# Seven-product query projection: two token blocks kept in place, output weights elsewhere, three value tiles moved behind the first products

## What is computed

```python
queries = (q @ Wq.T).reshape(B, Sq, NHEADS, HEAD_DIM).transpose(0, 2, 1, 3)
keys = (k @ Wk.T).reshape(B, Skv, KVHEADS, HEAD_DIM).transpose(0, 2, 1, 3)
values = (v @ Wv.T).reshape(B, Skv, KVHEADS, HEAD_DIM).transpose(0, 2, 1, 3)
queries = _rope(queries)
keys = _rope(keys)
...
attn = jax.nn.softmax(scores, axis=-1)
ctx = jnp.einsum('bhqk,bhkd->bhqd', attn, values)
ctx = ctx.transpose(0, 2, 1, 3).reshape(B, Sq, NHEADS * HEAD_DIM)
return ctx @ Wd.T
```

## Time and profile before

| what | value |
|---|---|
| median of 3 runs | 738.43 us (737.69 to 738.82) |
| the profiled execution | 738.54 us, of which the span is 736.7 us |
| granted TensorE clock, mean | 0.998 |
| TensorE busy | 710.8 us, 96% of the span |
| VectorE, GpSimd, ScalarE busy | 520.8, 485.9, 371.9 us |
| moved by DMA | 51.09 MB, mean 69 GB/s |

### The profile page before, as it was taken

One profiled execution on the slowest core, in us unless ns is written; L12 is line 12 of the kernel. 1 busy time (PEld: TensorE's weight loads), 2 busy tenths in 40 slices (PEclk: granted clock), 3 DMA queues, 4 the chain that ended last, 5 costly groups with the idle time before them and its releaser, 6 DMA issues.

```text
span 736.7 us, 12893 instructions
## 1 busy us (share of the span) xinstructions
PE 710.8 (96%) x4848; PEld 565.4 (77%) x4848; DVE 520.8 (71%) x815; ACT 371.9 (50%) x555; POOL 485.9 (66%) x366
## 2 busy tenths in 40 slices
PE   9999997799999999999999999989999999999897
PEld 7788886567787778787778778767787888877786
DVE  5756857766756757767757757757667887888855
ACT  5456645635544644743653554544246776653220
POOL 1898535678777776867867867746325799964440
PEclk9999999999999999999999999999999999999999
DMA  7553514031211310311301212200200110020003
GB/s 271 206 172 132 172 51 133 17 129 44 86 44 44 107 49 17 113 41 43 100 28 44 98 43 72 73 16 15 87 1 1 44 59 2 2 87 1 15 1 114
DMA packets 25561, 51.09 MB, mean 69 GB/s; under 512 B 2352, under 2 KB 10672, under 8 KB 25520
## 3 DMA queue, kind: packets, MB, share of 16 engines
q1 hardware_dynamic: 25520, 50.53, 20.8%
HBM read 40.04 MB, written 10.49 MB: 69 GB/s over the span
## 4 chain that ended last, share of the span: by engine, by line
PE 79%; DVE 7%; POOL 6%; ACT 3%; issue 3%; DMA 1%; SPq 0%; DVEq 0%; POOLq 0%
PE pj L1517 11%; PE sc L1610 9%; PE pj L1610 9%; PE pj L1708 8%; PE tp L1517 7%; PE pv L1503 6%; PE pv L1597 4%; PE tp L1610 4%; PE sc L1577 3%; PE tp L1491 2%; PE pj L1491 2%; PE sc L1758 2%; PE tp L1584 2%; PE tp L1771 2%; PE pv L1782 2%
## 5 line engine op out<-in xcount | busy, mean ns | idle before, releaser
L482 POOL TENSOR_TENSOR sw<-sw,cst 128x512 f32<-128x512 f32 x72 | 100.6, 1398 | 38.3 <-ACT sw L655 38.2
L1517 PE MATMUL pj<-x,w 128*128 128x512 f32 x384 | 103.5, 406 | 1.0 <-ACT pc L693 0.6
L506 POOL TENSOR_TENSOR sm<-sm,mx 128x512 f32<-128x512 f32 x64 | 72.0, 1131 | 45.5 <-DVE mx L1166 26.4
L1517 PEld LDWEIGHTS pj<-x,w 128*128 128x128 f32 x384 | 69.4, 189 | 24.6 <-DVE cq L1089 4.9
L500 POOL TENSOR_TENSOR w<-raw,w 128x896 fp32r<-128x896 f32 x28 | 60.9, 2196 | 34.6 <-ACT w L640 34.6
L511 POOL TENSOR_TENSOR sm<-sm,rz 128x512 f32<-128x512 f32 x64 | 65.9, 1043 | 19.5 <-DVE rz L1181 19.5
L1517 PE MATMUL tp<-x,w 128*128 128x512 f32 x288 | 76.2, 401 | 2.6 <-ACT sw L655 1.4
L488 POOL TENSOR_TENSOR qr<-t,sw 128x512 f32<-128x512 f32 x54 | 73.3, 1358 | 7.7
L775 ACT ACTIVATE sm<-sm 128x512 f32<-128x512 f32 x64 | 40.2, 631 | 69.2 <-POOL sm L506 69.2
L1708 PE MATMUL pj<-xh,ws 128*128 128x512 f32 x192 | 64.3, 401 | 0.2 <-ACT kb L863 0.2
L1517 PEld LDWEIGHTS tp<-x,w 128*128 128x128 f32 x288 | 51.9, 188 | 13.3 <-ACT sw L655 1.7
(11 more groups left out here) (268 smaller groups left out, 1799.3 us busy)
## 6 DMA issues: line engine op xcount, KB each, us to landing
rawd<-in_w_d SPq DMA_DIRECT2D x16, 512.0 KB, 3.3
raw<-in_w_q SPq DMA_DIRECT2D x15, 512.0 KB, 3.3
kscr<-sm SPq DMA_DIRECT2D x16, 256.0 KB, 2.2
vscr<-sm SPq DMA_DIRECT2D x16, 256.0 KB, 2.6
kr<-kscr SPq DMA_DIRECT2D x8, 512.0 KB, 3.3
vv<-vscr SPq DMA_DIRECT2D x16, 256.0 KB, 2.6
raw<-in_w_k SPq DMA_DIRECT2D x4, 512.0 KB, 6.2
cT<-in_ctxT SPq DMA_DIRECT2D x4, 512.0 KB, 7.4
```

The costliest lines, as they stand in the source:

```text
L482: pool.tensor_tensor(bs(sw[par][:, :]), bs(sw[par][:, :]), rep(cst[:, C_SIN:C_SIN + S], HB), ALU.mult).then_inc(sin_done, 1)
L506: pool.tensor_tensor(s3, s3, per_group(mx[:, c, :], 8), ALU.subtract).then_inc(subbed, 1)
L1517: last = pe.matmul(bank, a, r, start=(start and k == 0 and part == 0), stop=(stop and k == 1 and part == 2), skip_group_check=True)
```

## The change

Blocks 5 and 6 of the tokens are no longer in `x7`: their high and low parts are written into `xt`, which covers `cT`, on the quarters whose contents are no longer needed; the low part overwrites its own source. `wdh` and `wdl` take the place that these blocks had in `x7`, and the fourth `t1` temporary of the first queries becomes `t1x`, a place that value tiles 13 to 15 don't read. These three tiles go behind the first queries' products. `first_add(2)` and (3) come before (4) and (5), so head 0 waits for six sums instead of four. `w7_sum(2)` moves from between `block_lo(4)` and `block_lo(5)` to behind `first_t1(5)`. `kr` is loaded ahead of the last four value spills. A `memset` of `kb[0]`, which lies where `wdl` is now, waits for another count. The rest of the diff follows from these.

```diff
@@ -97,15 +97,17 @@
 
 
         xs = ExitStack()
-        x7 = sb(xs, "x7", [P, 7, 2, 1024], F32R)
+        x7 = sb(xs, "x7", [P, 5, 2, 1024], F32R)
+        wdh = sb(xs, "wdh", [P, REP, D], F32R)
+        wdl = sb(xs, "wdl", [P, REP, D], F32R)
         w7 = [sb(xs, f"w7{i}", [P, 2, 7 * 256], F32R) for i in range(2)]
         qr = sb(xs, "qr", [P, B, REP, S])
         kr = sb(xs, "kr", [P, B, S])
         cq = [sb(xs, f"cq{i}", [P, HALF]) for i in range(2)]
         u2 = sb(xs, "u2", [P, HALF])
         pc = sb(xs, "pc", [P, HALF])
-        wdh = sb(xs, "wdh", [P, REP, D], F32R)
-        wdl = sb(xs, "wdl", [P, REP, D], F32R)
+
+        xt = sb(xs, "xt", [P, KT, TOK], F32R)
         ch = sb(xs, "ch", [P, 2, 8, P], F32R)
         cl = sb(xs, "cl", [P, 2, 8, P], F32R)
         vv = sb(xs, "vv", [P, HB, DH])
@@ -132,6 +134,11 @@
         sb(f2, "gap_f2", [P, 100 * 256])
         raw8b = sb(f2, "raw8b", [P, 8, 256])
         f2.close()
+
+        f3 = ExitStack()
+        sb(f3, "gap_f3", [P, 136 * 256])
+        t1x = sb(f3, "t1x", [P, HALF])
+        f3.close()
         pcb, u2b = sm4[0], sm4[1]
         kst, vst = sm4[0:2], sm4[2:4]
 
@@ -273,6 +280,9 @@
         x7src = [xblock(0, 0), xblock(1, 0), xblock(1, 1), xblock(0, 0), xblock(1, 1), xblock(0, 1), xblock(1, 0)]
 
         def x7b(i, hl):
+            if i >= 5:
+                kh, h = (((1, 1), (0, 1)), ((0, 0), (1, 0)))[i - 5][hl]
+                return xt[:, 2 * kh:2 * kh + 2, h * HALF:(h + 1) * HALF]
             return x7[:, i, hl, :].rearrange("p (k t) -> p k t", k=2)
 
         def q_out(p, k):
@@ -325,7 +335,7 @@
 
         FIRST = [(0, 0), (1, 0), (0, 1), (1, 1), (0, 2), (1, 2), (0, 3), (1, 3)]
 
-        t1f, swf = t1 + pt, sw + swx
+        t1f, swf = t1 + [pt[0], t1x], sw + swx
 
         block = es.enter_context(nc.Block())
 
@@ -401,20 +411,21 @@
                     sp.wait_ge(wlo, 2)
                     sp.wait_ge(wsum, 6)
                     load_q(1, 0)
-
-            for i in range(2):
-                sp.wait_ge(s_ks[i], 16 * NKT // 2)
-            sp.wait_ge(wlo, 4)
-            load_kr(0)
+                if vi == 11:
+                    for i in range(2):
+                        sp.wait_ge(s_ks[i], 16 * NKT // 2)
+                    sp.wait_ge(wlo, 4)
+                    load_kr(0)
+
             sp.wait_ge(vproj, NVT)
             for i in range(2):
                 load_d(0, i)
+            sp.wait_ge(wlo, 6)
+            load_q(1, 1)
             for i in range(2):
                 sp.wait_ge(s_vs[i], 16 * NVT // 2)
             for i in range(2):
                 load_vv(0, i)
-            sp.wait_ge(wlo, 6)
-            load_q(1, 1)
 
             def head(g, last):
                 if not last:
@@ -536,8 +547,8 @@
                 first_add(i, i)
             for i in range(2, 6):
                 first_sin(i)
-            first_add(2, 4)
-            first_add(3, 5)
+            first_add(2, 2)
+            first_add(3, 3)
             first_sin(6)
             first_sin(7)
 
@@ -589,7 +600,7 @@
             late_lo(0)
             late_lo(1)
             late_lo(2)
-            pool.wait_ge(stp, 7 * N_PAIR)
+            pool.wait_ge(outx, 8 * (NKV - 1))
             pool.memset(kb[0][:, :, :, :], 0.0).then_inc(zeroed, 1)
             late_lo(3)
             ln_pow(2)
@@ -678,8 +689,8 @@
                     act.wait_ge(ln_cp, NT)
                 else:
                     act.wait_ge(tdone, (1, 3, 2, 4)[i - 3])
-                if i == 5:
-                    act.wait_ge(vproj, NVT)
+                if i >= 5:
+                    act.wait_ge(x_done, 5)
                 hi(x7src[i], x7b(i, 0), x7hi)
 
             def w7_hi(m, p, raw, free):
@@ -753,12 +764,9 @@
             first_swap(0, C_BANK)
             v_copy(12)
             first_swap(1, T_BANK)
-            v_copy(13)
+            block_hi(5)
             part_copy(u2, 5, A_BANK)
             part_copy(u2b, 6, B_BANK)
-            v_copy(14)
-            v_copy(15)
-            block_hi(5)
             block_hi(6)
             part_copy(pc, 7, C_BANK)
             part_copy(pcb, 8, T_BANK)
@@ -767,8 +775,11 @@
             first_swap(4, A_BANK, None, 1)
             first_swap(5, B_BANK, None, 2)
             w7_hi(2, 0, raw8, 13)
-            first_swap(6, C_BANK, None, 5)
-            first_swap(7, T_BANK, None, 6)
+            v_copy(13)
+            first_swap(6, C_BANK, None, 3)
+            v_copy(14)
+            first_swap(7, T_BANK, None, 4)
+            v_copy(15)
 
             def exp(n, c, scale):
                 act.wait_ge(subbed, n + 1)
@@ -1132,7 +1143,6 @@
                 dve.wait_ge(cadd, 1 + p)
                 first_t1(p, c)
             block_lo(4)
-            w7_sum(2)
             block_lo(5)
             block_lo(6)
             dve.wait_ge(wlo, 4)
@@ -1143,16 +1153,17 @@
             for p, a in enumerate((A_BANK, A2)):
                 dve.wait_ge(stp, 11 + p)
                 first_t1(4 + p, a, 1 + p)
-            first_add(4, 2)
+            w7_sum(2)
             c_add(13, 3, C_BANK, u2)
-            first_add(5, 3)
+            dve.wait_ge(cadd, 5)
+            first_t1(6, C_BANK, 3)
+            first_add(4, 4)
+            first_add(5, 5)
+            c_add(14, 4, C2, u2b)
+            dve.wait_ge(cadd, 6)
+            first_t1(7, C2, 4)
             w7_lo(2, 0, 0)
-            c_add(14, 4, C2, u2b)
-            dve.wait_ge(cadd, 5)
-            first_t1(6, C_BANK, 5)
             w7_lo(2, 0, 1)
-            dve.wait_ge(cadd, 6)
-            first_t1(7, C2, 6)
             first_add(6, 6)
             first_add(7, 7)
             for i in range(2):
@@ -1512,7 +1523,7 @@
             def product(bank, p, w, xb, start, stop):
                 for k in range(2):
                     wh, wl = (w7[p][:, i, w * 256 + k * P:w * 256 + (k + 1) * P] for i in range(2))
-                    mh, ml = (x7[:, xb, i, k * HALF:(k + 1) * HALF] for i in range(2))
+                    mh, ml = (x7b(xb, i)[:, k, :] for i in range(2))
                     for part, (a, r) in enumerate(((wh, mh), (wh, ml), (wl, mh))):
                         last = pe.matmul(bank, a, r, start=(start and k == 0 and part == 0),
                                          stop=(stop and k == 1 and part == 2), skip_group_check=True)
@@ -1541,13 +1552,10 @@
                 product(a, p, W_11, X_11, True, False).then_inc(stp, 1)
                 product(c, p, W_12, X_21, True, True).then_inc(stp, 1)
             v_tile(12)
-            v_tile(13)
             for p, a in enumerate((A_BANK, A2)):
                 pe.wait_ge(x_done, 5)
                 pe.wait_ge(pcp, 1 + p)
                 product(a, p, W_S2, X_T2, False, False).then_inc(stp, 1)
-            v_tile(14)
-            v_tile(15)
             for p, c in enumerate((C_BANK, C2)):
                 pe.wait_ge(swp, Q0 + 1 + p)
                 product(c, p, W_S1, X_T1, True, False).then_inc(stp, 1)
@@ -1562,6 +1570,8 @@
             for p, c in enumerate((C_BANK, C2)):
                 pe.wait_ge(pcp, 5 + p)
                 product(c, p, W_S4, X_22, False, True).then_inc(stp, 1)
+            for i in range(13, NVT):
+                v_tile(i)
 
             def scores_x(g, j, held=False):
                 h, c = j // 2, j % 2
@@ -1620,7 +1630,7 @@
                     pe.wait_ge(x_done, XD0 + 8 * g + j + 1)
 
                 m = 2 * n
-                pe.wait_ge(rope, Q0 + 4 if first else ri(m, 0))
+                pe.wait_ge(rope, Q0 + 6 if first else ri(m, 0))
                 pe.wait_ge(s_kr, 16 * (g + 1))
                 scores_x(g, 0)
                 scores_x(g, 1)
```

## The result

The changed kernel took 732.73 us (median of 6 runs, 731.85 to 733.41), the kernel before, beside it, 738.44 (737.59 to 739.23): a ratio of 0.9923, 95% interval 0.991 to 0.9936. Forecast were 731.0 us, 729.6 to 734.4, and a gain of 7.5 us; the gain is 5.7. The sign and the mechanism came out, the size was 1.8 us too large. The time lies in the range, but 0.2 above what I had given for case A (729.6 to 732.5) and so in the part that I had given to rival B, the chain that doesn't compress. What that says is worked out behind the experiments.

What follows compares the result with a forecast made beforehand. TensorE's idle time, with head 0's first mask on VectorE as the instruction that sets S1, was taken as the bound. Mask at 123.4 for 130.91, 7.5 us earlier: 738.5 - 7.5 = 731.0 us, range 729.6 to 734.4.

Steps and rivals of the forecast that it cites:

- case A: The forecast itself: first mask at 123.4 for 130.91, 7.5 us gained; 729.6 to 732.5 us, chance 0.68.
- rival B: Chain from `c_add` to `first_add(7)` hides nothing, `w7_sum` adds 4.6: gain 3.7 us; 732.5 to 736.9, chance 0.22.
- What bounds it: TensorE's idle time around head 0's start; VectorE's first mask, at 130.91, sets S1 7.40 us later.
- Parts 1 and 2: Value tiles 13 to 15 behind S4, blocks 5 and 6 written elsewhere: S3 at 102.9, 8.4 us earlier.
- part 2: Token blocks 5 and 6 written where the tokens lie, `block_lo` 1.22 us each: costs nothing, covered by S1's 2.72.
- Rival D: Matmuls reading blocks 5 and 6 from their new place cost more; 0.1 us each gives 750; chance 0.04.
- Part 3: Rotary chain on VectorE moves 8.4 us earlier with S3; `w7_sum(2)` put in takes 4.65; `first_add(7)` done at 122.9.
- Part 4: ScalarE's queue: `v_copy(15)` ends at 120.7, last value spill lands at 123.3 and decides the mask by 0.4 us.
- Part 5: SP's loads: `kr` earlier at no cost; others land between 125 and 130, `w_q` with under 2 us to spare.
- The sum: First mask 7.5 us earlier, S1 at 130.8, shift kept to the end: 738.5 - 7.5 = 731.0 us.
- The rule that I weighed: VectorE operations with two SBUF inputs and GpSimd SBUF reads exclude each other: `w7_sum` stage 0.7 later, total 731.7 us.

Runs made afterwards that it cites:

- q_first: best with SP's load of pair 3's weights (read by `w7_sum(3)`) moved ahead of the last value spill; 730.70 us, ratio 0.9898.
- sum_back: Changed kernel with `w7_sum(2)` back between `block_lo(4)` and `block_lo(5)`; 733.35 us, ratio 0.9928.
- rope_back: Changed kernel with the rotary sums in the old order, 4 and 5 ahead of 2 and 3; 732.69 us, ratio 0.9918.
- after_again: The changed kernel unaltered, measured once more; 733.05 us, ratio 0.9906 to the kernel before.
- sum_pool_adds: Changed kernel with `w7_sum(2)`'s three additions on GpSimd and `first_add(2)` and (3) on VectorE; 733.22 us, ratio 0.9921.
- best: sum_pool_adds with VectorE's spill wait ahead of mask 2, `first_swap(7)` ahead of `v_copy(14)`, and half of `w7_lo(2)` on GpSimd; 732.93 us, ratio 0.9903.
- v_back: Changed kernel with value tiles 13 to 15 and their ScalarE copies at their old places; 740.94 us, ratio 1.0025.
- fill_hole: Kernel before with 12 matmuls that nobody reads in TensorE's idle time behind S4; 739.37 us, ratio 0.9989.

## Why the prediction was right, and where it was short

**What bounds it: right, and the step that carried the most.** The forecast took one instruction, the first mask, and a fixed distance of 7.40 to S1. Every kernel but `q_first`, where a load came between, gave 7.40 to 7.42. That TensorE keeps the shift from there on was right: 6.56 us at S1, 6.62 at 651 us.

**Parts 1 and 2: right to 0.1 us on TensorE, part 2 with some luck.** S3, S4 and the first scores came where they were put, and tile 15 didn't wait. Rival D, dearer matmuls at the new place, has nothing to rest on: the 24 matmuls took 5.44 us as before, and the shift was 6.56 us at S1 and 6.62 at 651 us, with all the heads between. The two `block_lo`, put at 1.22 each, took 4.05 together, by the same neglect as in part 3; TensorE's work covered it. In `sum_back`, where they start later, S3 waited 1.04 us for them.

**Part 3: the term that was mis-sized.** I took the long durations for `w7_sum`, because GpSimd was busy, and the short ones (0.7) for the four `first_add` behind it, although they read two buffers of the same memory just as it does. `first_add(4)` and (5) took 2.61 for 1.4, and (6) 1.78 for 0.7. `w7_lo` gave 0.7 back. `w7_sum` was 0.75 shorter than I took it, which bought nothing, as VectorE then waited 0.65 and 0.80 us for GpSimd's sums; `first_add(4)` started at 115.87 for 116.0. In sum VectorE's queue was done at 124.26 where I had 122.9, and the mask, which I had put at 123.4 for the spill, was 0.9 late, or 1.1 from the first product on.

Between A and B: from the `c_add` for k=1 to the end of `first_add(7)` the chain took 124.34 - 104.53 = 19.8 us. It was 17.9 before, and the 3.9 of `w7_sum` came on top, so 2.0 us of it was hidden, where A needed 4.3 (22.5 less 18.2) and B had none. The measured chain lies about midway, and so does the time at the border of the two ranges: that the total fell inside the stated range owes something to its width. My early argument against rival B, that the new order takes VectorE's additions out of the chain, was wrong in its reason: `rope_back` lost nothing.

**Part 4: right in kind.** The spill was to decide by 0.4 us. It was in 0.01 us before the mask in one execution and held it up by 0.53 in the other. It was 1.0 later than put (124.33 for 123.3) because `first_t1(7)`, and with it swap 7 and `v_copy(15)` (121.67 for 120.7), was late, not for a reason of its own.

**Part 5: right, with the warning that mattered.** No load was late in the changed kernel: `w_q` was issued at 123.15, took 6.2 us to land and was read at 130.39, 1.0 us later. With a mask 0.3 earlier it was already waited for, since it took 8.0 us to land in `sum_back`, and it became the bound with the mask 1.9 us earlier.

```profile
130.68 0.42 DVE L1063 TENSOR_TENSOR raw<-raw 128x256 f32<-128x256 f32 x1 [0.78 <-DMA raw<-in_w_q]
```

**The sum: the other microsecond.** 7.5 - 0.9 = 6.6 stood at 651 us. The last 0.98 went to a stretch of half clock that in the profiled execution before had fallen into idle time. I had read that stretch as costing nothing, which was right, and hadn't asked where the next would fall. That is the account of two profiled executions. Over many it isn't shown that closing the hole costs a microsecond: the kernel before mostly has a stretch behind its hole as well, and in the second comparison, `after_again`, the gain was 739.74 - 733.05 = 6.7 us, which is what the chain gave. The two ratios' intervals overlap (0.991 to 0.9936 and 0.9892 to 0.992), so the size of this term stays open between nothing and about 1 us.

The rule that I weighed, of the page "SBUF — State Buffer" of the Trainium skill ("Who interferes with whom"), bears on the missed term: it names every VectorE operation with two inputs in SBUF, beside a GpSimd operation that reads SBUF, and not `w7_sum` alone. The traces agree: operations of 128x512 took 0.69 us alone and 1.65 to 1.78 beside GpSimd. The 0.7 us that I had for the rule isn't worked out in the forecast. What the additions of the chain lost beside GpSimd is 1.2 + 1.1 = 2.3 us.

## What to carry to other kernels

Moving work that isn't needed yet (here three tiles, 8.2 us) from ahead of a long serial chain to behind its head starts the chain that much earlier, and fills the time in which the bound engine waits for it. What it is worth is what the last instruction of the chain moves: 6.6 of the 8.2 us here. Find the one instruction through which the stage's end is tied, check that its distance to the bound engine is fixed, and forecast that instruction. And when pricing a chain on VectorE, go through GpSimd's timeline beside it, operation by operation: take the long duration for each pair with inputs in the same memory, not just for the one that was moved.

## What the runs showed that I had not expected

A stretch at the lower of TensorE's two levels (1.2 GHz for 2.4) came behind 140 us in twelve of the fourteen profiled executions (not in the kernel before, and not in `sum_pool_adds`, whose mean clock was 1.00), in places that differ between executions of one kernel (651 us; 490 and 681 us). But over all kernels the starts of these stretches lie in only three places: 489 to 498, 649 to 652 and 679 to 689 us. `best` and `v_back` have one more each, behind the idle time ahead of 140 us. Ahead of each, TensorE had little to do for some microseconds. Windows of the changed kernel, and then of `after_again`, just before their stretches:

```profile
648.00:651.40 3.40, 1.77 (x17) 1.09 (x12) 3.30 (x7) 1.19 (x2) 3.40 (x4) 1.00 0.91 267
```
```profile
487.00:490.60 3.60, 1.49 (x19) 0.98 (x19) 3.46 (x4) 1.04 (x2) 1.35 (x2) 1.00 0.04 15
...
678.30:681.70 3.40, 1.51 (x12) 1.26 (x12) 3.40 (x4) 1.27 (x3) 2.18 (x1) 1.00 0.28 82
```

Little work doesn't decide it by itself: in the changed kernel TensorE was busy 0.94 of 3.00 us from 487 to 490, and the clock stayed at 1.00 behind it. Why one execution falls at one place and the next at another stays open. Where profiles were compared, each stretch behind 140 us cost about 1 us, and the one in the old hole nothing. In `fill_hole` the three timed runs with a mean clock of 1.00 took 737.9 to 738.4 us, and those at 0.995 took 738.7 to 740.3. The clock isn't all of the scatter: `best` took 731.0 and 734.5 us at the same mean clock of 0.995. That is more than most of the variants differ by, so with this kernel tenths are to be read from profiles, aligned at a common instruction, and with a second profile of the same kernel beside them: the spill alone moved S1 by 0.5 us.
